# A four-block conv and FFN kernel: another way to the router's pixel means in the front of the last FFN

## The reference

```python
logits = jnp.mean(x, axis=1) @ Wr + br                  # one row of 8 experts for each image
routing_weights = jax.nn.softmax(logits, axis=-1)
capacity = float(math.ceil(N * CAPACITY_FACTOR / E))
expected_loads = routing_weights.sum(axis=0) * (N / B)
scale = jnp.where(expected_loads > capacity, capacity / expected_loads, 1.0)
routing_weights = jax.nn.softmax(routing_weights * scale, axis=-1)
...
top_w, top_i = jax.lax.top_k(rw_tok, K)                 # K = 2, the same for all tokens of an image
top_w = jax.nn.softmax(top_w, axis=-1)
...
out = _layer_norm(out + x, gamma, beta)
```

## Time and profile before

| | |
|---|---|
| median of 3 runs | 676.01 us (674.55 to 680.59) |
| the profiled execution | 678.35 us, of which the span is 676.6 us |
| mean granted clock of TensorE in it | 0.93 |
| TensorE busy | 593.2 us (88%) |
| VectorE, ScalarE, GpSimd busy | 431.5 (64%), 353.0 (52%), 305.0 us (45%) |

### The profile page before, as it was taken

One profiled execution on the slowest core, in us unless ns is written; L12 is line 12 of the kernel. 1 busy time (PEld: TensorE's weight loads), 2 busy tenths in 40 slices (PEclk: granted clock), 3 DMA queues, 4 the chain that ended last, 5 costly groups with the idle time before them and its releaser, 6 DMA issues.

```text
span 676.6 us, 11644 instructions
## 1 busy us (share of the span) xinstructions
PE 593.2 (88%) x3608; PEld 383.7 (57%) x3608; DVE 431.5 (64%) x1262; ACT 353.0 (52%) x729; POOL 305.0 (45%) x395
## 2 busy tenths in 40 slices
PE   7898794876999998998998888989899999998883
PEld 6685334874555564554555668974444554467652
DVE  6645597778797786776868854857533333434557
ACT  4334686276534443434435545555466666435384
POOL 6502655230544457858648921621333333335153
PEclk9997895597999999999999898999899999996697
DMA  4810000203435234225321000113222222000001
GB/s 114 146 25 1 2 0 1 57 7 88 107 70 123 67 90 97 62 63 117 70 63 31 1 2 1 31 30 102 64 62 63 62 63 70 24 2 1 1 1 63
DMA packets 24853, 34.62 MB, mean 51 GB/s; under 512 B 11048, under 2 KB 20288, under 8 KB 22816
## 3 DMA queue, kind: packets, MB, share of 16 engines
q1 hardware_dynamic: 24800, 33.95, 21.3%
HBM read 32.50 MB, written 1.44 MB: 50 GB/s over the span
## 4 chain that ended last, share of the span: by engine, by line
PE 43%; DVE 11%; POOL 9%; issue 3%; ACT 2%; DMA 1%; DVEq 0%; SPq 0%; POOLq 0%; ACTq 0%
PE ps L1837 10%; PE ps L2464 8%; PE ps L2480 7%; PE ps L1881 5%; POOL out_acc L1485 3%; POOL dw_out L1603 3%; PE ps L2586 2%; POOL tap_prod L1613 2%; PE ps L2895 1%; PE ps L1621 1%; PE ps L421 1%; DVE ST L487 1%; PE ps L2217 1%; PE ps L2906 1%; DVE tok_tmp L1739 1%
## 5 line engine op out<-in xcount | busy, mean ns | idle before, releaser
L1485 POOL TENSOR_TENSOR out_acc<-out_acc,tok_tmp 128x512 f32<-128x512 f32 x80 | 103.7, 1296 | 197.6 <-DVE tok_tmp L2398 101.2
L1837 PE MATMUL ps<-tokT,w 128*128 128x512 f32 x512 | 135.7, 409 | 5.3 <-ACT act_buf L1796 2.7
L1796 ACT ACTIVATE act_buf<-ps 128x512 f32<-128x512 f32 x128 | 75.6, 598 | 95.9 <-PE ps L1837 91.1
L1837 PEld LDWEIGHTS ps<-tokT,w 128*128 128x128 f32 x512 | 92.2, 190 | 54.9 <-issue 24.3
L2464 PE MATMUL ps<-tokT,w 128*128 128x512 f32 x256 | 69.6, 414 | 1.1 <-ACT hid_buf L2445 1.1
L2464 PEld LDWEIGHTS ps<-tokT,w 128*128 128x128 f32 x256 | 46.2, 191 | 28.5 <-ACT hid_buf L2445 13.5
L1734 DVE TENSOR_TENSOR hid_buf<-act_buf,ps 128x512 f32<-128x512 f32 x64 | 43.3, 685 | 20.8 <-ACT act_buf L1796 15.6
L1734 DVE TENSOR_TENSOR tok_split<-act_buf,ps 128x512 f32<-128x512 f32 x64 | 43.0, 684 | 18.1 <-ACT act_buf L1796 17.1
L532 ACT ACTIVATE U<-X,nmr,rstd 128x64 f32<-128x64 f32 x116 | 40.4, 428 | 23.8 <-POOL nmr L510 17.4
L2445 ACT ACTIVATE hid_buf<-ps,b 128x512 f32<-128x512 f32 x64 | 38.9, 683 | 22.2 <-PE ps L2464 22.1
L2445 ACT ACTIVATE tok_split<-ps,b 128x512 f32<-128x512 f32 x64 | 38.8, 691 | 15.2 <-PE ps L2464 14.7
(11 more groups left out here) (474 smaller groups left out, 1098.5 us busy)
## 6 DMA issues: line engine op xcount, KB each, us to landing
disp_all<-disp_dram SPq DMA_DIRECT2D x30, 512.0 KB, 6.3
disp_all<-disp_dram SPq DMA_DIRECT2D x30, 256.0 KB, 3.9
w_raw<-in_L_ffn_w SPq DMA_DIRECT2D x4, 512.0 KB, 9.3
XIN<-in_x SPq DMA_DIRECT2D x4, 256.0 KB, 3.6
w_raw<-in_L_ffn_W SPq DMA_DIRECT2D x2, 512.0 KB, 6.1
out<-XIN SPq DMA_DIRECT2D x4, 256.0 KB, 2.2
disp_all<-disp_dram SPq DMA_DIRECT2D x6, 128.0 KB, 3.0
disp_all<-disp_dram SPq DMA_DIRECT2D x2, 384.0 KB, 5.0
```

Of the source, the lines that this page charges most:

```text
L1485: pool.tensor_tensor(out_acc[:, :], out_acc[:, :], weighed[p % 2], ALU.add).then_inc(mm["acc"].sem, 1)
L1796: act.activation(act_buf[e % 2][:, :], ps[:, e % 2, :], ACT.Silu).then_inc(mm["act"].sem, 1)
L1837: last = pe.matmul(ps[:, 2 * k + e % 2, :], w12[:, part, k, EXPERT1[e], :], tokT[:, bass.ts(i, CHUNK)], start=(part == 0), stop=(part == 1))
```

## The change

The one-column products are removed. For groups 0 to 2 VectorE sums the copied tokP over the pixels (`tensor_reduce`, 512 elements to 2 sums); for group 3 ScalarE copies in two halves that also give their sums (`accum_out`). mean8 is scaled from these sums in SBUF. The transposes of the four groups go to four separate banks (0, 1, 5, 6), and TensorE's wait for an earlier copy goes. The first softmax takes the minimum of the negated logits, and the exponential negates again, with the minimum as its bias; both exponentials give their sums. The load product has the constant 256 / capacity as its weights in place of ones, so that two VectorE instructions remain behind it; the second softmax no longer subtracts a maximum. The constant products are placed anew: 8 ahead of group 1, 4 ahead of groups 2 and 3, 8 behind group 3 ahead of the logits, and 30 instead of 10 behind the load product.

```diff
--- before.py
+++ after.py
@@ -308,6 +308,8 @@
         b2_8 = sb("b2_8", [E3, C], region="last")
         mean8 = sb("mean8", [P, B], region="last")
         im = [sb(f"im{i}", [B, E3], region="last") for i in range(8)]
+        pair_sums = sb("pair_sums", [P, B // 2], region="last")
+        load_part = sb("load_part", [B, B], region="last")
         i1 = [sb(f"i1_{i}", [B, 1], region="last") for i in range(4)]
         hot = sb("hot", [B, 2, E3], region="last")
         iw = sb("iw", [B, 2, 2], region="last")
@@ -2666,11 +2668,12 @@
 
 
         I_BY_DVE = (0, TG // 2, TG // 2, TG // 2)
-        HB, SUM, BACK = (2, 3, 4, 5), (6, 1), (7, 0)
+        HB, SUM, BACK, I_BANK = (2, 3, 4, 5), (6, 1), (7, 0), (0, 1, 5, 6)
 
         def i_vector(dve):
 
             wwait(dve, "i8")
+            dve.memset(load_part[:, :], float(PIX) / float(CAP))
             vlink(dve.memset(mean8[:, :], 0.0))
             for g in range(G):
                 dve.wait_ge(*m["i_rstd"](g + 1))
@@ -2682,29 +2685,27 @@
                     last = dve.tensor_scalar(U[:, tt, :], X[:, tt, :], rstd[:, tt:tt + 1], nmr[:, tt:tt + 1], ALU.mult, ALU.add)
                 last.then_inc(m["i_fs"].sem, 1)
 
-            dve.wait_ge(*m["i_sum"](1))
+            for g in range(G - 1):
+                dve.wait_ge(*m["i_ft"](g + 1))
+                last = dve.tensor_reduce(pair_sums[:, 2 * g:2 * g + 2], tokP[:, g * CHUNK:(g + 1) * CHUNK].rearrange("p (q s) -> p q s", q=2),
+                                         X_AXIS, ALU.add)
+            vlink(last)
+            dve.wait_ge(*m["i_ft"](G))
             for r in range(2):
-                last = dve.tensor_scalar(mean8[half(r), :].rearrange("p (q r) -> p r q", r=2)[:, r, :], ps[half(r), 3, C:C + B // 2],
+                last = dve.tensor_scalar(mean8[half(r), :].rearrange("p (q r) -> p r q", r=2)[:, r, :], pair_sums[half(r), :],
                                          1.0 / PIX, None, ALU.mult)
             last.then_inc(m["i_mean"].sem, 1)
             dve.wait_ge(*m["i_lg_ps"](1))
-            vlink(dve.tensor_tensor(im[0][:, :], ps[0:B, 3, 0:E3], br_8[:, :], ALU.add))
-            vlink(dve.tensor_reduce(i1[0][:, :], im[0][:, :], X_AXIS, ALU.max))
-            dve.tensor_scalar(im[1][:, :], im[0][:, :], i1[0][:, :], None, ALU.subtract).then_inc(m["i_l"].sem, 1)
+            vlink(dve.scalar_tensor_tensor(im[0][:, :], ps[0:B, 3, 0:E3], -1.0, br_8[:, :], ALU.mult, ALU.subtract))
+            dve.tensor_reduce(i1[0][:, :], im[0][:, :], X_AXIS, ALU.min).then_inc(m["i_l"].sem, 1)
             dve.wait_ge(*m["i_e"](1))
-            vlink(dve.tensor_reduce(i1[0][:, :], im[2][:, :], X_AXIS, ALU.add))
-            vlink(dve.reciprocal(i1[1][:, :], i1[0][:, :]))
+            vlink(dve.reciprocal(i1[1][:, :], i1[2][:, :]))
             dve.tensor_scalar(im[3][:, :], im[2][:, :], i1[1][:, :], None, ALU.mult).then_inc(m["i_rw"].sem, 1)
 
             dve.wait_ge(*m["i_ld_ps"](1))
-            vlink(dve.tensor_scalar(im[4][:, :], ps[0:B, 3, 0:E3], float(PIX), None, ALU.mult))
-            vlink(dve.reciprocal(im[5][:, :], im[4][:, :]))
-            vlink(dve.tensor_scalar(im[4][:, :], im[5][:, :], float(CAP), 1.0, ALU.mult, ALU.min))
-            vlink(dve.tensor_tensor(im[0][:, :], im[3][:, :], im[4][:, :], ALU.mult))
-            vlink(dve.tensor_reduce(i1[0][:, :], im[0][:, :], X_AXIS, ALU.max))
-            dve.tensor_scalar(im[1][:, :], im[0][:, :], i1[0][:, :], None, ALU.subtract).then_inc(m["i_l2"].sem, 1)
+            vlink(dve.reciprocal(im[5][:, :], ps[0:B, 3, 0:E3]))
+            dve.scalar_tensor_tensor(im[1][:, :], im[5][:, :], 1.0, im[3][:, :], ALU.min, ALU.mult).then_inc(m["i_l2"].sem, 1)
             dve.wait_ge(*m["i_e2"](1))
-            vlink(dve.tensor_reduce(i1[0][:, :], im[2][:, :], X_AXIS, ALU.add))
             vlink(dve.reciprocal(i1[1][:, :], i1[0][:, :]))
             vlink(dve.tensor_scalar(im[3][:, :], im[2][:, :], i1[1][:, :], None, ALU.mult))
 
@@ -2792,16 +2793,22 @@
             def pairs(g):
 
                 act.wait_ge(*m["i_ft_ps"](g + 1))
-                act.activation(tokP[:, g * CHUNK:(g + 1) * CHUNK], ps[:, g % 2, :], ACT.Copy).then_inc(m["i_ft"].sem, 1)
+                if g < G - 1:
+                    act.activation(tokP[:, g * CHUNK:(g + 1) * CHUNK], ps[:, I_BANK[g], :], ACT.Copy).then_inc(m["i_ft"].sem, 1)
+                    return
+                for q in (2 * g, 2 * g + 1):
+                    last = act.activation(tokP[:, q * PIX:(q + 1) * PIX], ps[:, I_BANK[g], q % 2 * PIX:(q % 2 + 1) * PIX], ACT.Copy,
+                                          accum_out=pair_sums[:, q:q + 1])
+                last.then_inc(m["i_ft"].sem, 1)
             ln_norm(act, 0, m["i_rstd"], m["i_u"], by_dve=I_BY_DVE[0])
             for g in range(G):
                 if g + 1 < G:
                     ln_norm(act, g + 1, m["i_rstd"], m["i_u"], by_dve=I_BY_DVE[g + 1])
                 pairs(g)
             act.wait_ge(*m["i_l"](1))
-            act.activation(im[2][:, :], im[1][:, :], ACT.Exp).then_inc(m["i_e"].sem, 1)
+            act.activation(im[2][:, :], im[0][:, :], ACT.Exp, bias=i1[0][:, :], scale=-1.0, accum_out=i1[2][:, :]).then_inc(m["i_e"].sem, 1)
             act.wait_ge(*m["i_l2"](1))
-            act.activation(im[2][:, :], im[1][:, :], ACT.Exp).then_inc(m["i_e2"].sem, 1)
+            act.activation(im[2][:, :], im[1][:, :], ACT.Exp, accum_out=i1[0][:, :]).then_inc(m["i_e2"].sem, 1)
             act.wait_ge(*m["i_w"](1))
             act.activation(i1[1][:, :], i1[0][:, :], ACT.Exp).then_inc(m["i_we"].sem, 1)
             act.wait_ge(*m["i_ready"](1))
@@ -2847,27 +2854,22 @@
         def i_tensor(pe):
 
             for g in range(G):
-                keep_clock(pe, 4, 12 if g == 0 else 2)
+                keep_clock(pe, 4, 12 if g == 0 else 8 if g == 1 else 4)
                 pe.wait_ge(*m["i_u"](g + 1))
                 if I_BY_DVE[g]:
                     pe.wait_ge(*m["i_fs"](g + 1))
-                if g >= 2:
-                    pe.wait_ge(*m["i_ft"](g - 1))
-                elif g == 0:
+                if g == 0:
                     pe.wait_ge(*m["q_xp"](G))
                 for i in range(4):
-                    last = pe.transpose(ps[:, g % 2, i * P:(i + 1) * P], pair(U, g * TG + 2 * i), ident[:, :])
+                    last = pe.transpose(ps[:, I_BANK[g], i * P:(i + 1) * P], pair(U, g * TG + 2 * i), ident[:, :])
                 last.then_inc(m["i_ft_ps"].sem, 1)
-                for i in range(4):
-                    at = C + 2 * g + i // 2
-                    last = pe.matmul(ps[:, 3, at:at + 1], pair(U, g * TG + 2 * i), ones[:, 0:1], start=(i % 2 == 0), stop=(i % 2 == 1))
-            last.then_inc(m["i_sum"].sem, 1)
+            keep_clock(pe, 4, 8)
             pe.wait_ge(*m["i_mean"](1))
             wwait(pe, "i8")
             pe.matmul(ps[0:B, 3, 0:E3], mean8[:, :], wr_8[:, :], start=True, stop=True).then_inc(m["i_lg_ps"].sem, 1)
             pe.wait_ge(*m["i_rw"](1))
-            pe.matmul(ps[0:B, 3, 0:E3], ones[0:B, 0:B], im[3][:, :], start=True, stop=True).then_inc(m["i_ld_ps"].sem, 1)
-            keep_clock(pe, 4, 10)
+            pe.matmul(ps[0:B, 3, 0:E3], load_part[:, :], im[3][:, :], start=True, stop=True).then_inc(m["i_ld_ps"].sem, 1)
+            keep_clock(pe, 4, 30)
             pe.wait_ge(*m["i_top"](1))
             for k in range(2):
                 pe.transpose(ps[0:E3, 2, k * B:(k + 1) * B], hot[:, k, :], ident[0:B, 0:B])
```

## The result

The changed kernel takes 683.1 us in the median of ten runs (679.82 to 684.86), the kernel before 677.25 beside it (674.55 to 683.29): a ratio of 1.0061, 95% interval 1.0032 to 1.0090. Timed again with twelve runs against twenty, it was 680.43 against 679.06, 1.0031 (1.0007 to 1.0054). So it is slower by 0.3 to 0.6%, where 670.7 and a gain of 0.8% had been forecast. Both are under the 1% that the prediction called hardly measurable, but both intervals leave out 1, on the other side than forecast, and 683.1 lies above the range of 667.9 to 675. The profiled execution took 684.02 us, with a span of 682.3.

The account below looks back on a forecast made before the run. The prediction took TensorE at half clock in the front of the last FFN as the bound. Gains of 4.2 + 0.3 + 0.8 = 5.3 us, off the 676.01 median, gave 670.7, range 667.9 to 675.

Parts of the forecast that it names:

- the prediction's 619.3: End of group 3's two ScalarE copies with accumulator reads, put at 0.9 us from 618.4.
- signs of being right: Clock 1.00 from 611 to 629, logits near 620.0, constant products ending after `dia`, no ScalarE idle before the first exponential.
- The means take the 0.42 that they take now.: Front's end: the means would take 0.42 us, the present time from last product to logits, ending at 619.7.
- The 30 constant products behind the load product: Ahead of the transposes of `hot`: these products, not VectorE, end last, at 628.4; `hot` gains 4.2 us.
- 60 instructions at 0.112: Full-clock price of the 30 constant products behind the load product: from 621.7 to 628.4.
- the rival of the fall in the relay: Clock falls from 620.25 to 621.7, so constant products start at half clock; `hot` at 630.4, total 672.7; chance 0.22.
- the slower rival: Clock falls in the front all the same and the 30 products bind: 677.2, or 682.5 if it stays low; chance 0.11.
- Behind `hot`: From `hot` onward: 0.3 us (0 to 1.0) ahead of the experts, 0.8 (0 to 1.57) in the first sixteen expert products.
- The sum: Whole gain: 4.2 up to `hot`, plus 0.3 and 0.8 behind it, 5.3 us.

Follow-up runs that it names:

- e3_both: Changed kernel with 10 instead of 30 constant products behind the load product and the means formed by a reduction over one element; ratio to the kernel before 0.9957.
- e2_one_port: Changed kernel with the means formed by a reduction over one element, the division by 256 moved into the logits' scalar, 30 products kept; ratio to before 0.9988.
- e12_adds_late: Changed kernel with GpSimd's four additions moved out of the front, behind its weight picks; mean's form and 30 products kept; median 681.58 us, ratio to before 1.0053.
- e9: Changed kernel, unchanged, profiled a second time; span ends 66.10 us behind the first transposes of U; no timed ratio.
- e10: Changed kernel, unchanged, profiled a third time; span ends 64.71 us behind the first transposes of U; no timed ratio.
- e11: Changed kernel, unchanged, timed again beside the kernel before; 680.43 against 679.06 us, ratio 1.0031.
- e1: Changed kernel with 10 instead of 30 constant products behind the load product; ratio to the kernel before 0.9967.
- e5: Changed kernel with the constant products placed as in the kernel before, so the new sums and softmax alone; ratio to before 0.9965.
- e7: Changed kernel with means by one-element reduction and constant products fitted into TensorE's waits (4, 23 and 3, and 8 ahead of the experts); ratio to before 0.9953.
- e8_before_again: Kernel before, unchanged, profiled once more; span ends 64.40 us behind the first transposes of U; no timed ratio.
- e6_products_only: Kernel before with the constant products placed and numbered as in the changed kernel, nothing else; median 679.82 us, ratio to before 1.0044.

## Why the prediction was wrong

**What held.** The clock stayed at 1.00 through the front. The last copy ended at 624.36 + 0.85 = 625.21, 7.6 behind U; the prediction's 619.3 is 7.74 behind its U. The reduces were hidden, the accumulator read of the exponential took 0.18 for 0.21, and the table load ended at 626.49, before it was wanted. From the logits to the end of `dia` it took 16.93 - 9.99 = 6.94 us, forecast 7.05. With the mean mended (e3_both) the logits came at 8.46 and the load product at 10.00, where 8.44 and 10.0 had been forecast. The products did end last, and not VectorE. Three of its signs of being right failed: the logits came 9.99 behind U in place of 8.44, the clock did not stay at 1.00 until the products had ended, and ScalarE stood idle for 1.71 us between the table load and the first exponential, since the mean was late.

**"The means take the 0.42 that they take now."** This step failed. The row was of a mean that read PSUM, at 624.04, when GpSimd's additions were over (617.81 to 622.75), as the timeline of the kernel before shows:

```profile
617.81 4.94 POOL L2646 TENSOR_TENSOR X<-X,bet 128x512 f32<-128x512 f32 x4 [1.75 <-ACT U L532]
...
624.06 0.34 DVE L2687 TENSOR_SCALAR mean<-ps 64x8 f32<-64x8 f32 x2 [6.98 <-PE ps L2863]
```

The new one goes from SBUF to SBUF and stands among them. It took 2.22 us, since each of its two instructions ended with a running addition; in another form (e2_one_port) or without the neighbour (e12_adds_late) it took 0.33 and 0.35. The prediction asked only which engine ends last, and not what GpSimd does in those microseconds. The Trainium skill, "SBUF — State Buffer", section "Who interferes with whom", says that VectorE's `tensor_scalar` can take the port pair that it shares with GpSimd, that the one that issues first holds the pair for a whole instruction while the other "fully blocks", and that `tensor_reduce` never contends on trn2. The rows of 625.31 and 626.32, the 0.33 of e2_one_port and the two copies of 1.14 and 1.20 us in e12_adds_late all agree. Price on the path: 9.99 - 8.46 = 1.53 us at the logits.

**"The 30 constant products behind the load product": "60 instructions at 0.112".** The mechanism was right, the term mis-sized: 8.59 us, and 9.85 in another execution, for the 6.7 of the sum. The wait for the mean left TensorE nearly idle from 626.1 to 629.2, and 18 of the 60 went at half clock. In all six profiles with the late mean (after, e9, e10, e11, e1, e5) the clock fell between the start of the mean and `hot`, 9.4 to 13.0 us behind U; in the four without it (e2, e3, e7, e12) it did not fall until `hot` was issued. At full clock the 60 took 6.96 (e2_one_port, e12_adds_late). This is the rival of the fall in the relay, which had 18 at half and `hot` 18.84 behind U; with the 1.53 of the mean on top that makes 20.4, and 20.15 was measured. It was given 0.22 with an idle time of about 1.45 us in view (620.25 to 621.7); the mean made it 3.1. What the prediction had as the slower rival, a fall in the front, did not happen. Even at full clock these products bind by 1.1 to 1.6 us (e2_one_port, e12_adds_late; forecast 1.35); with ten of them (e1_ten, e3_both) VectorE releases `hot`.

**"Behind `hot`": 0.3 + 0.8.** The first term held: from `hot` to the first expert products it took 4.07 us in place of 4.73, so 0.66 was won where 0.3 (0 to 1.0) had been put. The second failed, its sign included. The clock was full when `hot` was issued and fell again at 640.6, behind 2.80 us in which TensorE was busy for 1.70; the first sixteen expert products took 4.28 us in place of 3.69, and the eight output products behind them 1.7 in place of 1.1. From `hot` to the end it took 44.56 us, 0.57 more than before (43.99). Only e7_fit, with products in that wait as well, kept the clock.

**The sum.** In the first profiles the change won 0.90 us up to `hot` (forecast 4.2) and lost 0.57 behind it (forecast a gain of 1.1): 0.33 of 5.3. Of the 3.31 us that `hot` came too late, 1.51 stood at the load product already (11.50 for 9.99 behind U) and the rest in the 60 instructions (8.59 for 6.72). The sums alone are worth 4 to 5 us of path (e5_sums_only); the products put to them take 3.13 of it back up to `hot` (17.02 to 20.15) and 4.4 up to the end (60.35 to 64.71), so hardly anything is left.

**What stays open.** Behind U the four profiles of after are 0.4 us longer in the mean than the two of before (65.1 and 64.7), while the medians say 2.1 to 4.1 us. And the seven kernels with the new sums of which a timed ratio can be set against a tail (e1, e2, e3, e5, e7, e11, e12) all did worse in the median than behind U, against the 64.7 of before: by 1.6 to 2.6 us, and e12 by 5.3. These steps take the gain away; they do not make the kernel slower than before.

The granted clock points to the stretch ahead of the last FFN. U starts at 614.5 in the mean of the ten profiles with the new sums and at 612.8 in the four without, but it ranges from 612.2 to 617.6 and from 611.0 to 616.8, and on the whole it comes later the longer the clock was at 0.50 ahead of it. In two executions of the kernel before it was at 0.50 for 61.4 us and 75.1 us ahead of U, with U at 611.56 and 616.80. One stretch of each, 370 to 500, in the columns above, first before, then e8_before_again:

```profile
370.00:500.00 130.00, 115.64 (x701) 84.34 (x701) 81.97 (x205) 68.88 (x134) 49.05 (x56) 0.95 0.15 38
370.00:500.00 130.00, 114.63 (x693) 85.25 (x695) 80.77 (x204) 67.96 (x132) 50.77 (x57) 0.92 0.14 35
```

A straight line through all fourteen profiles gives U 0.32 us for each us at half clock. For the timed runs this allows an estimate. Their mean clock (0.9307 in the twenty runs of before beside e11_after_timed; 0.9350 in its own twelve and 0.9308 in the first ten of the changed kernel) and their span give all their time at half clock: 94, 88 and 94 us. The profiles have 33 us of it behind U in the kernel before and 22 in the changed one. That leaves about 60, 66 and 72 us ahead of U, and at 0.32 the changed kernel loses about 2 and 4 us there, the size of what the medians say. So the remainder seems to lie ahead of the last FFN and to go with the clock there. Why the changed kernel, whose instructions up to U are the same by the diff, should be at half clock longer, no run shows, and this stays open; the executions that were profiled may also simply be other draws of the clock than the timed ones, as in e6_products_only.

## What to carry to other kernels

When an operand moves from PSUM to SBUF, look in the timeline at what GpSimd does in those microseconds, not only at who ends last; a small VectorE instruction beside long GpSimd ones is best given a form that does not wait for them, as the reduction over one element did not here. Constant products that are to hold the clock stand in the issue order ahead of real work: let none run past the end of the wait that they fill. Thirty in one place cost 3.2 us of path; ten there, or thirty spread over three waits (e7_fit), did not, and the medians of these two don't tell them apart. And where the clock falls is another matter in each execution, so compare profiles from a mark inside them, and look at several.

## What was not expected of the hardware

A 64x8 instruction of VectorE took 1.00 and 1.22 us beside GpSimd's additions of 1.27 us, where two took 0.35 without them; one of 16x8 with two operands in SBUF took 0.70 in place of 0.15. U starts 5.2 us apart in two executions of the same program (611.56 and 616.80 for the kernel before). The accumulator reads behind the copies are cheap: two copies of 256 columns with their reads took 0.85 us, less than the 0.9 put down.
